# A graph attention kernel: TensorE's order of 36 steps rewritten with value products in pieces of one to four quarters

## The reference

```
q = (x @ Wq.T).reshape(d, n, h)      # d = 128 heads, n = 3327, h = 8
k = (x @ Wk.T).reshape(d, n, h)
v = (x @ Wv.T).reshape(d, n, h)
a = einsum('dnh,dmh->dnm', q, k) * scale
a = a + adj + adj
a = softmax(a, axis=2)
out = einsum('dnm,dmh->dnh', a, v)
x = x + out.reshape(n, h*d) @ Wo.T
```

## Time and profile before

| what | value |
|---|---|
| median of three runs | 13,902.25 us |
| the profiled execution's span | 13,904.2 us |
| TensorE busy (matmul) | 13,474.1 us, 97% |
| VectorE busy | 13,175.3 us, 95% |
| ScalarE busy | 13,116.0 us, 94% |
| GpSimd busy | 1,509.8 us, 11% |
| DMA | mean 148 GB/s |
| mean granted TensorE clock | 0.992 |

### The profile page before, as it was taken

One profiled execution on the slowest core, in us unless ns is written; L12 is line 12 of the kernel. 1 busy time (PEld: TensorE's weight loads), 2 busy tenths in 40 slices (PEclk: granted clock), 3 DMA queues, 4 the chain that ended last, 5 costly groups with the idle time before them and its releaser, 6 DMA issues. The chain is left out here.

```text
span 13904.2 us, 337069 instructions
## 1 busy us (share of the span) xinstructions
PE 13474.1 (97%) x130699; PEld 4162.7 (30%) x130699; DVE 13175.3 (95%) x27486; ACT 13116.0 (94%) x26756; POOL 1509.8 (11%) x1220
## 2 busy tenths in 40 slices
PE   5989999999999999999999999999999999999998
PEld 3522222222222222222222222222222222222224
DVE  6689999999999999999999999999999999999992
ACT  2379999999999999999999999999999999999997
POOL 2220101111110111111111111111111111111110
PEclk8999999999999999999999999999999999999999
DMA  8975656656565655656566565656656565665653
GB/s 285 254 158 140 148 139 145 142 138 149 139 149 138 146 142 138 149 137 149 138 145 143 138 149 137 149 139 143 144 138 150 138 149 137 145 143 139 148 138 92
DMA packets 1951493, 2060.35 MB, mean 148 GB/s; under 512 B 756537, under 2 KB 1704800, under 8 KB 1943488
## 3 DMA queue, kind: packets, MB, share of 16 engines
q1 hardware_dynamic: 1949062, 2035.58, 62.4%
q10 hardware_dynamic: 824, 3.21, 0.1%
HBM read 1929.05 MB, written 109.05 MB: 147 GB/s over the span
## 5 line engine op out<-in xcount | busy, mean ns | idle before, releaser
L239 DVE CUSTOM_DVE_ANT_0 swept<-X,adj_row 128x832 f32<-128x832 f32 x13312 | 12838.9, 1021 | 349.5 <-PE X L261 282.4
L1000 ACT ACTIVATE prob<-S 128x476 f32<-128x476 f32 x23296 | 11598.4, 569 | 155.0 <-PE S L1068 43.7
L1090 PE MATMUL O<-prob,v_pad 128*32 128x238 f32 (+1 forms) x77648 | 6677.1, 416 | 21.8 <-ACT o_sb L1026 19.1
L1068 PE MATMUL S<-q_blk,k_res 60*128 60x476 f16 x23296 | 5963.2, 368 | 35.9 <-DVE q_blk L1037 15.2
L261 PE MATMUL X<-mk,mq 40*128 40x416 f16 x26624 | 5757.7, 344 | 153.1 <-DVE m_part L239 80.5
L1068 PEld LDWEIGHTS S<-q_blk,k_res 60*128 60x128 f16 x23296 | 1666.6, 93 | 3512.7 <-ACT prob L1000 1476.9
L261 PEld LDWEIGHTS X<-mk,mq 40*128 40x128 f16 x26624 | 1541.8, 93 | 3244.4 <-DVE m_part L239 2729.2
L1090 PEld LDWEIGHTS O<-prob,v_pad 128*32 128x32 f32 x77648 | 1528.5, 108 | 2661.9 <-issue 2403.2
L991 ACT ACTIVATE S<-adj_key 128x476 f32<-128x476 f32 (+1 forms) x2912 | 1701.2, 584 | 35.0 <-issue 4.3
L211 POOL TENSOR_SCALAR m_neg<-m_full 128x16 f32<-128x16 f32 x208 | 52.5, 253 | 11327.4 <-DVE m_full L222 11327.2
L961 POOL TENSOR_SCALAR q_blk<-q_blk 24x1904 f16<-24x1904 f16 (+1 forms) x222 | 1108.4, 4993 | 142.9 <-DMA q_blk<-q_planes 126.0
(11 more groups left out here) (85 smaller groups left out, 1059.1 us busy)
## 6 DMA issues: line engine op xcount, KB each, us to landing
adj_row<-in_adj SPq DMA_DIRECT2D x1600, 416.0 KB, 3.8
adj_key<-adj_by_key SPq DMA_DIRECT2D x2496, 238.0 KB, 3.9
mk<-k_planes SPq DMA_DIRECT2D x1664, 104.0 KB
adj_key<-adj_by_key SPq DMA_DIRECT2D x416, 236.0 KB, 3.9
mk<-k_planes SPq DMA_DIRECT2D x1664, 52.0 KB
row<-in_adj SPq DMA_DIRECT2D x47, 1663.5 KB, 8.2
adj_by_key<-aT SPq DMA_DIRECT2D x26, 1664.0 KB, 12.0
mq<-q_planes SPq DMA_DIRECT2D x416, 64.0 KB
```

Source lines behind the costliest of these rows:

```text
L239: nc.vector.tensor_tensor_reduce(out=swept[u % 2][:], in0=x_, in1=adj_row[gi % 4][:].rearrange("p (a b) -> p a b", a=2), scale=1.0, scalar ...
L1000: nc.scalar.activation(prob[born(j, d // 4) % QR][:, d % 4, 0:w], S[b][:, 0:w], ACT.Exp, scale=2.0).then_inc(s_e[b], 1)
L1068: nc.tensor.matmul(S[b][:, 0:w], k_res[base:base + KR, d // 2, s * P:(s + 1) * P], q_blk[n % 2][base:base + KR, d // 2, 0:w], start=False, ...
L1090: done = nc.tensor.matmul(O[32 * d:32 * d + 32, cols], v_pad[:, s, 4 * q + d, :], prob[born(j, q) % QR][:, d, cols], start=first, stop=Tru ...
```

## The change: what it does

`ORDER` is written anew. Letters `a`, `b`, `c`, `d` take the place of `v` and `V`; they stand for one, two, three and four quarters of a quad's width (119, 238, 357 and 476 queries). A letter may begin anywhere in a quad, and where it reaches over the quad's end `values` issues two pieces, each with its own 8 matmuls. The letters of scores and units have other places too; there are still 36 steps with 72 scores, 41 units and 72 quarters. `HELD` is 15 for 14, so that value work runs one half later. `s_pv` counts quarters, and `place` and the waits for it are scaled with that.

```
-    ORDER = ("xy01", "v0x1", "yv0x1", "yv0xy1", "vxy01", "xyv01", "xyv01", "xyv0x1", "y0vxy1", "0xy1", "Vxy01", "xy0Vxy1",
-             "xy01", "v0x1", "yv0x1", "yv0xy1", "vxy01", "xyv01", "xyv01", "xyv0x1", "y0vxy1", "0xy1", "Vxy01", "xy0Vxy1",
-             "x01", "yv0xy1", "0v1", "xyx01", "yV0x1", "yv0xy1", "v0x1", "y0xyv1", "0x1", "yv0x1", "yVxy01", "xy0vxy1v")
+    ORDER = ("cxy01", "abxy01", "0xyaaa1", "0xy1", "bxy01", "xycx01", "ybx01", "yb0x1", "yaxy01", "b0x1", "ydxy01", "xy0dxy1",
+             "xy01", "b0x1", "yb0x1", "ya0x1", "yc0x1", "yc0xy1", "ax0y1", "a0x1", "ya0xy1", "b0x1", "yabxy01", "x0ycxy1",
+             "xy01", "bx0y1", "b01", "xyaaxy01", "bxyaxy01", "bxy01", "bx01", "ybx01", "ya0x1", "ybx01", "yabxy0x1", "y01xy")
-    HELD = 14
+    HELD = 15
...
+                def quarters(letter):
+                    return " abcdefgh".index(letter)
                 def place(h):
-                    cycle, i = divmod(h + HELD, CYCLE)
+                    cycle, i = divmod(2 * (h + HELD) + 1, 2 * CYCLE)
                     fills = done = 0
                     for letter in "".join(ORDER):
-                        fills += letter in "01"
-                        done += " vV".index(letter) if letter in "vV" else 0
+                        if letter in "01":
+                            fills += 1
+                        elif letter not in "xy":
+                            done += quarters(letter)
                         if done > i:
                             return 2 * CYCLE * cycle + fills
...
-                                        wait(sp, s_pv, 2 * rank_of(j, 1) + 2)
+                                        wait(sp, s_pv, 4 * rank_of(j, 1) + 4)
...
-                                act.wait_ge(s_pv, 104 * (n + 1))
+                                act.wait_ge(s_pv, 208 * (n + 1))
...
-                            cols = slice(0, w) if wide == 2 else slice(w // 2 * h, w // 2 * (h + 1))
+                            cols = slice(w // 4 * r, w // 4 * (r + count))
                             for d in range(4):
                                 done = nc.tensor.matmul(O[32 * d:32 * d + 32, cols], v_pad[:, s, 4 * q + d, :], prob[born(j, q) % QR][:, d, cols],
                                                         start=first, stop=True, skip_group_check=True)
-                            done.then_inc(s_pv, wide)
+                            done.then_inc(s_pv, count)
+                        def values(part, count):
+                            at, end = max(part, 0), min(part + count, 2 * STEPS)
+                            while at < end:
+                                n = min(end - at, 4 - at % 4)
+                                part_values(at // 4, at % 4, n)
+                                at += n
...
-                                    wide = 2 if letter == "V" else 1
-                                    values(half, wide)
-                                    half += wide
+                                    values(part, quarters(letter))
+                                    part += quarters(letter)
```

More of the change, by code:

```diff
@@ L1069, in scores, with part_values @@
                                              start=False, stop=True, skip_group_check=True).then_inc(s_s[b], 1)
[L1071 to L1075, removed]
+                        def part_values(rank, r, count):
                             j, q = quad_of(rank)
@@ L1078, in values @@
                             w = width(n)
-                            first = rank % (2 * NT) == 0 and h == 0
+                            first = rank % (2 * NT) == 0 and r == 0
                             if first and n:
                                 pe.wait_ge(s_oc, n)
-                            if h == 0:
+                            if r == 0:
                                 if n % NBL == 0 and q == 0:
@@ L1091, in values @@
                                                         start=first, stop=True, skip_group_check=True)
-                            done.then_inc(s_pv, wide)
+                            done.then_inc(s_pv, count)
[5 more added lines that the diff above has]
+                                at += n
                         for c in range(CYCLES):
-                            fill, unit, half = 2 * CYCLE * c, LEAD + TURN * c, CYCLE * c - HELD
+                            fill, unit, part = 2 * CYCLE * c, LEAD + TURN * c, 2 * (CYCLE * c - HELD)
                             for letter in "".join(ORDER):
```

## The result

The changed kernel takes 14,022.3 us (median of four runs, 14,020.7 to 14,032.1) against 13,902.0: a ratio of 1.0088, with a 95% interval of 1.0075 to 1.0101. That is +120 us where +153 were forecast.

What follows compares the result with a forecast made beforehand. VectorE's sweeps were taken as the bound, 39.05 of 40.2 us a cycle, with TensorE close behind. From 13,902 us, +91 for the running balance and +63 for blocks' ends gave 14,056, stated as 14,055; 8-in-10 range 13,740 to 14,230.

Steps and rivals of the forecast that it cites:

- likeliest case: The prediction's own forecast for the whole kernel: 14,055 us, 1.1% slower, range 13,960 to 14,190, chance 0.50.
- The letters' price: TensorE's value pieces and the stretches between them: 0.75 us more work a cycle of 36 steps, bounds -0.05 to 2.1.
- the joint: Extra TensorE time where two value pieces meet inside a run: taken as 0.054 us, 15 a cycle, 0.8 us.
- The running balance: TensorE's price between units less 0.952 us a sweep: VectorE loses 1.01 us a cycle for 0.73, +91 us.
- 0 for it: ScalarE's share of the change, TensorE's waits for it being alike: taken as 0, bounds -160 to +160 us.
- The mean distance of sweeps: Sign in VectorE's trace: the mean distance between sweeps should rise from 0.982 to about 0.99 us.
- TensorE's waits for sweeps and exponentials: Sign in TensorE's trace: the forecast would be wrong if these shrank by more than 1 us a cycle.
- the letters' sum: TensorE's work for 36 steps without waits: 37.75 us before, leaving 2.45 of 40.2 for waits; 38.5 after.
- The ends of blocks: TensorE waiting for ScalarE's copy of O: 1.1 us for 0.25 at 74 of 111 ends, +63 us, 0 to 80.
- Passes bound by their loads: Rival on TensorE's quarter passes: weight loads add 1.4 us a cycle, about +450 us, 14,350; chance 0.08.
- TensorE's extra work hides in its waits, and only the blocks' ends stay: Rival: TensorE's waits absorb the added work and block ends are partly covered, 13,900 to 13,965 us; chance 0.12.
- The faster case: Rival: finer pieces starve ScalarE and VectorE less, half of 1.2 us a cycle returns, 13,770 us; chance 0.30.

Runs made afterwards that it cites:

- e1: Changed kernel, but a new block's first piece directly behind the old block's last is issued ahead of the next value letter: 13,901.0 us, 1.0001 against before.
- e4: Kernel before, its order with every half value letter cut into two quarter pieces at the same place, `HELD` 14: 13,934.0 us, 1.0025.
- e6: e1 with the value letters of steps 17 to 20 made even: 13,944.9 us, 1.0032 against the kernel before, 44 us above e1.
- e7: Kernel before with its latest unit (step 28) issued ahead of the value piece of step 27: 13,967.3 us, 1.0048.
- e5: Changed kernel with the value letters of steps 17 to 20 made even: 14,049.8 us, 1.0108 against the kernel before.
- e8: Kernel before with each block's last value piece held back to directly ahead of the next block's first, all 111 ends: 14,060.3 us, 1.0115.
- e11: e1 with a new block's first piece held back to the next value letter at all nine places of ends: 13,908.4 us, 1.0007 against before.

## Why the prediction was right, and where its parts were not

The direction, the place on the page and the sum were right: +153 forecast, +120 measured, inside the likeliest case's own range. That the sum came so near was luck: one term was far too high, another was half of what it should be, and the two made up for each other.

**The letters' price.** The 0.75 us a cycle more for TensorE, from which the balance was worked out, was far too high. The pieces were as forecast (0.34 and 0.35 for a lone quarter, 0.145 for a run), only the joint is 0.01 and not 0.054; at 15 of them this is 0.66 us less, which leaves about 0.1 us a cycle. I had the lower bound from the earlier trace rows, 4 ns, and chose a value in between; the row of the nearest kind was the answer.

**The running balance, +91 us: this is the step that failed.** e1 puts it at 0, with an interval of -11 to +14 us. The balance named the late units of the new order well: those behind the `c` of step 18 (0.32 us by the balance, 0.31 in the mean of after's trace), behind the `c` of step 17 (0.13 and 0.15), in step 11 (0.19 and 0.28) and in step 5 (0.12 and 0.09) are those that are late. Without the ends, in e1's trace, they are 0.23, 0.15, 0.19 and 0.09 late. It did not follow that the cycle is longer than before. Take the lateness over 0.945 us of each of the 41 sweeps of a cycle, its median over all cycles, and add them up (sweeps with another operation of VectorE ahead of them left out): before has 1.10 us and e1 1.06, where the balance had 0.73 and 1.01. It missed 0.37 us of the old order and 0.05 of the new one, whose joints it had priced too high; the difference of its two sums was the forecast. The same sum is 1.18 in e4, 1.18 in e6 and 1.33 in e7; against before, e1 and before, times 324, that is 26, 39 and 75 us, near the 34, 43 and 67 measured.

To leave ScalarE out, with "0 for it", was the likely fault: the three banks of S tie a score to the third exponential before, and in e6 that decided where the time went. That the 0.37 us are ScalarE's is not shown. e5 to e7 show three times, each time against the balance's sign, that making one unit earlier makes others later.

**The signs it named.** The mean distance of sweeps rose to 0.992 us as forecast, but not for the balance's reason: in e1 it is 0.982 again. TensorE's waits for sweeps and exponentials were not to shrink by more than 1 us a cycle. In the weight loads' rows they did, by 1,073 us or 3.3 a cycle; but those rows have 13 us a cycle before, where the letters' sum leaves 2.45 for waits, so they cannot decide this. With the joints at 0.01 the letters' sum leaves 2.4 in e1 too.

**The ends of blocks, +63 us.** The mechanism was right and its size half of what it was: 119 us by e1. Two things are missing in my 1.1 us. The copy starts 0.5 to 1.0 us after the last piece's end at these places (73 ends, not 74) and not 0.3, because ScalarE has instructions ahead of it; before, it starts 0.07 to 0.48 us after the piece at all 111 ends. The mean over the six places is 0.8, and 0.5 x 73 = 37 us. And the clock falls. Between 1,000 and 13,600 us, at the five places of the order that have drops, 27 blocks start with one and 33 without; compared place by place, by the distances of the copies of O, those with a drop last 1.9 us longer in the mean and 1.6 by the medians. That makes an estimate of 42 to 51 us, if the drop is their cause and not only their mark. With 63 and 37 these are 142 to 151, some 20 to 25% more than the 119 measured; that VectorE's and ScalarE's lead covers the rest is likely and not shown.

**The rivals.** Passes bound by their loads are excluded by e4 and by the lone quarter's 0.35 us; the Trainium skill's surcharge for narrow load and matmul pairs (TensorE: Matmul & The Clock Gate, "Back-to-back issue gap") does not appear in these float32 passes of 119 columns on four column tiles: with that page's 25 ns more (81 for 56) on each of its two passes a lone quarter would take 0.39 us by estimate. "TensorE's extra work hides in its waits, and only the blocks' ends stay" was nearest to the truth for the cycle, and I gave it 0.12, though there was little to hide: 0.1 us a cycle by the letters. Its time was too low because the ends were priced too low. The faster case did not come: with the ends out of the runs, in e1, the new letters gain nothing.

## What to carry to other kernels

In an in-order queue that three engines share, ask first for the rare event that stands in the pattern: here 6 of 9 places of an end that comes once in 104 steps cost all of the 0.9%, while the 60% more pieces of the new order cost nothing that could be measured (e4's 80% more, in the old order, cost 34 us). Where a resource is handed over (a PSUM bank that must be copied out), keep other work between its last use and its next, and price the wait with what is queued ahead of the copy on the copying engine. A list of late instructions isn't a list of losses: take the lateness away in one and see the others before it is counted.

## What the runs showed of the hardware

- In the middle of dense work TensorE's granted clock fell to its lower level, 1.2 GHz, for 3.4 to 10 us in 27 of the 73 cases of after's trace in which 1.4 to 1.9 us lay between the start of the last matmul and that of the next; behind the 111 gaps of the kernel before at the same kind of place, 0.27 to 0.9 us, never. Such a gap is not the only way to a drop: of e8's ten, two came at gaps of 1.1 us, and one of them, e1's one and e11's three came with no gap over 0.93 us in the 12 us before them. What sets it off stays open. The forecast had no term for it.
- A float32 value product on four column tiles costs its columns (1.667 ns each) and 0.145 us for each run of them between scores and units, but only about 0.01 us for another piece, with its own weights, inside the run: loads recorded with 109 ns do not lengthen passes of 99 ns.
